# The last two row tiles as a block pair, with their conversions moved, in a quantised feed-forward kernel

## Chip, cores and metric

One core of a Trainium2 chip. The metric is the device time of one execution in microseconds (us), the median of several runs.

## The reference

The input `x` has 2 x 2048 rows of 512, in 32 tiles of 128 rows. For each batch element a weight matrix is mixed from eight, `x` is multiplied by it and a bias is added; the result goes through a gated feed-forward block whose three weight matrices are ternary and whose activations are rounded to 8 bits with a scale per row; the block's output is added to `x`.

```python
w_bot = einsum('bg,got->bot', cond_8, weight * mask)
h = einsum('bnt,bot->bno', x, w_bot) + bias
act_quant(v): s = 127 / max|v| over the row;  round(v * s) / s
weight_quant(w): s = 1 / mean|w|;  clip(round(w * s), -1, 1) / s
gate = silu(act_quant(h) @ weight_quant(w_gate).T)
up = act_quant(h) @ weight_quant(w_up).T
out = x + act_quant(gate * up) @ weight_quant(w_down).T
```

## The kernel before

Everything is written out by hand: five programs, one for each engine's queue (PE, DVE, ACT, POOL and SP), which meet through semaphores only. An instruction that waits holds up everything behind it on its engine.

**Conditioning (up to about 119 us).** For every row tile `h = x @ w_bot + bias` is formed in fp32. Tiles 0 to 7 are done plainly: four products of 128 x 512 a tile (`cond_products`, L1126), then on DVE the bias sum, the largest absolute value of each row and two small operations (`cond_tile`, L871 to L879), then on ACT rounding (L546, adding and later taking away the constant ROUND) and conversion to fp16 (L541), then a DMA transpose by SP into `qT` (L256). Tiles 8 to 29 go as eleven *block pairs* (`pair_product`, L1308): two tiles and the halves of their matrices are multiplied as a 2 x 2 block product with seven block products instead of eight, each two instructions of 128 x 256 columns. For this POOL forms four sums of the input blocks (`pair_sum`, L414), ACT puts the bias into PSUM (`seed_bias`, L557) and copies the first product (`copy_first`, L564), and DVE adds shared parts between products (`pair_share` L891, `pair_seed` L898, `pair_c22` L904) and takes the largest values of both tiles in one reduction (`pair_largest`, L911). The weights are made ternary beside it: scaling on POOL (L398) or, for w_down, on ACT (`scale_down`, L568), then two passes on DVE (`ternary_piece`, L862 and L864), four pieces for each matrix.

Tiles 30 and 31 (`LATE` = 30) are not part of this. Their products are plain, eight slices that are put between the chunks of steps 0 to 2.

**Steps 0 to 31 (from 119 us).** Step s takes tile s through gate and up: four chunks of 512 columns, each a gate product (L1164), an up product (L1171), a SiLU on ACT (`silu_chunk`, L593) and a multiplication on DVE (`product`, L988). DVE then reduces the largest value (`largest`, L1006), forms the scale (L1048, L1051, L1053), and ACT rounds the tile (`round_tile`, L623) and converts it in two halves (`convert`, L640). SP transposes each half into `q2T` (L321). From step 6 on the gate side too is done in block pairs (L1206). The down products (L1236) go as block pairs of two tiles, seven products spread over the following steps; their sums of blocks are formed on DVE (`add_blocks`, L954) as soon as both tiles are transposed, and four combinations of w_down's blocks are formed once on POOL (L446 to L451, into `combo`). Then POOL has two unit columns (`unit_of`, L455), eight combinations of w_gate's blocks for each half (`combine_gate`, L372 to L377), and for every step the unit, the sums of `qT` blocks (L493) and the output tile (L462 to L473). DVE's scale (L1048) of step s waits for the unit of step s - 2.

**The end.** Tile 30 and tile 31 are multiplied by w_down plainly (`down_plain` L1243, `down_cut` L1253), between the last products of pair 14. Tile 30 is rounded in two halves (`round_half`, L629); the first is converted on POOL (`convert_first_half`, L498), the second on ACT. Tile 31 is rounded on DVE (L1060) and converted on ACT.

## Time and profile before

| | us |
|---|---|
| median of 3 runs | 440.59 |
| lowest and highest run | 439.86 to 440.75 |
| the profiled execution, its own time | 440.59 |
| span of the profiled execution | 438.8 |
| PE busy in the span | 425.5 |
| DVE, ACT, POOL busy | 363.5, 336.8, 205.3 |

The span runs from the first to the last instruction that the profiler recorded; 1.8 us of the execution's own time lie around it. PE is TensorE, DVE VectorE, ACT ScalarE, POOL GpSimd, SP the engine that issues most DMAs. In a timeline row stand the start in us from the span's start, the duration, the engine, the line, the operation and its operands; in square brackets the time for which the engine had nothing to do before, and what ended it. An fp32 product stands there as two instructions.

### The profile page before, as it was taken

To read this page: it belongs to the slowest core of one execution; us is meant where nothing else is said; L and a number is where in the kernel's file an instruction comes from. 1 tells how busy PE (TensorE), PEld (TensorE's weight loads), DVE (VectorE), ACT (ScalarE), POOL (GpSimd) and SP (SyncE) were. 2 spreads that over 40 slices of the span, in tenths; PEclk is the share of its full clock that TensorE was granted. 3 is DMA by queue.
4 is the path that set the end of the run, shared out by engine and by line. 5 is a ranking of instruction groups with operands and counts; after the bars stand their busy time and mean duration, and the time that the engine had idled before them with its cause. 6 is when DMAs were issued, how large, how long until landed. Compare 5 with 4: busy or idle time off the path is not lost.

```text
span 438.8 us, 7668 instructions
## 1 busy us (share of the span) xinstructions
PE 425.5 (97%) x2318; PEld 257.5 (59%) x2318; DVE 363.5 (83%) x611; ACT 336.8 (77%) x474; POOL 205.3 (47%) x221
## 2 busy tenths in 40 slices
PE   4899999999999999999999999999999999999997
PEld 0234688888744455556555565655566555556555
DVE  0327768898897988899999999899999999899992
ACT  1215988778867976888888888888888888888871
POOL 0006999999149995142432423344142333414132
PEclk9999999999999999999999999999999999999999
DMA  7999999995142337254453635535263553535375
GB/s 277 404 396 408 308 335 339 313 251 144 36 98 48 61 66 187 48 145 85 134 120 73 146 70 143 97 118 120 76 157 64 135 115 100 120 87 142 80 162 154
DMA packets 104458, 69.79 MB, mean 159 GB/s; under 512 B 87280, under 2 KB 87536, under 8 KB 102896
## 3 DMA queue, kind: packets, MB, share of 16 engines
q1 hardware_dynamic: 103712, 67.13, 56.9%
q10 hardware_dynamic: 720, 2.36, 1.5%
q8 instruction: 11, 0.18, 0.2%
q14 instruction: 15, 0.12, 0.1%
HBM read 40.11 MB, written 8.39 MB: 111 GB/s over the span
## 4 chain that ended last, share of the span: by engine, by line
PE 59%; DMA 14%; issue 11%; DVE 9%; ACT 5%; POOL 1%; DVEq 0%; ACTq 0%; SPq 0%; POOLq 0%
PE ps L1308 15%; DMA wc<-wc 12%; PE ps L1171 11%; PE ps L1236 10%; PE ps L1126 8%; PE ps L1206 8%; PE ps L1164 4%; ACT wc L640 3%; DVE wc L954 3%; DVE wc L988 2%; DMA wc<-wcond 2%; PE ps L1139 2%; DVE p_part L1006 1%; ACT result L660 1%; PE ps L1243 1%
## 5 line engine op out<-in xcount | busy, mean ns | idle before, releaser
L1171 PE MATMUL ps<-tern_up,qT 128*128 128x512 f16 x512 | 131.1, 379 | 0.0
L1171 PEld LDWEIGHTS ps<-tern_up,qT 128*128 (+1 forms) x512 | 50.0, 98 | 54.5 <-DVE wc L988 0.4
L1006 DVE TENSOR_REDUCE p_part<-wc 128x1 f32<-128x1536 f32 x64 | 77.9, 1217 | 1.7
L988 DVE TENSOR_TENSOR wc<-ps,xT_sb 128x512 f32<-128x512 f32 x104 | 71.1, 683 | 7.3 <-issue 3.3
L640 ACT ACTIVATE wc<-wc 128x1024 f16<-128x1024 f32 x63 | 66.0, 1051 | 4.1 <-DMA wc<-wc 2.1
L623 ACT ACTIVATE wc<-wc,p_scale 128x2048 f32<-128x2048 f32 x30 | 60.1, 2002 | 4.3 <-DVE p_scale L1053 4.3
L1236 PE MATMUL ps<-wc 128*128 128x256 f16 x480 | 62.2, 273 | 0.7 <-DVE wc L954 0.7
L954 DVE TENSOR_TENSOR wc<-wc 128x1024 f16<-128x1024 f16 x60 | 56.9, 949 | 4.5 <-DMA wc<-wc 3.6
L1236 PEld LDWEIGHTS ps<-wc 128*128 128x128 f16 x480 | 46.9, 98 | 18.6 <-issue 1.2
L455 POOL TENSOR_SCALAR out_unit<-p_max,up_step,w_mean 128x1 f32<-128x1 f32 x32 | 11.3, 355 | 99.2 <-DVE p_max L1048 99.2
L618 ACT ACTIVATE xT_sb<-ps,gate_unit 128x512 f32<-128x512 f32 x78 | 49.2, 683 | 10.9 <-PE ps L1206 10.4
L462 POOL TENSOR_TENSOR result<-result,x_res 128x512 f32<-128x512 f32 x15 | 19.1, 1273 | 73.3 <-issue 73.3
L1236 PE MATMUL ps<-tern_down,wc 128*128 128x256 f16 x360 | 46.7, 273 | 0.6 <-ACT ps L653 0.5
L1236 PEld LDWEIGHTS ps<-tern_down,wc 128*128 128x128 f16 x360 | 35.1, 98 | 14.6 <-ACT ps L653 0.7
L1126 PE MATMUL ps<-w_bot,xT_sb 128*128 128x512 f32 x80 | 36.7, 597 | 1.6 <-DVE w_bot L845 1.6
L1206 PE MATMUL ps<-tern_gate,qT 128*128 128x512 f16 x104 | 26.7, 379 | 0.0
L1126 PEld LDWEIGHTS ps<-w_bot,xT_sb 128*128 128x128 f32 x80 | 14.9, 190 | 19.6 <-issue 15.9
L593 ACT ACTIVATE wc<-ps,gate_unit 128x512 f32<-128x512 f32 x24 | 16.2, 683 | 12.6 <-PE ps L1164 12.6
L837 DVE SCALAR_TENSOR_TENSOR w_bot<-ps,half_on,w_bot 128x512 f32<-128x512 f32 x8 | 6.0, 747 | 23.4 <-PE ps L1139 23.4
L1164 PE MATMUL ps<-tern_gate,qT 128*128 128x512 f16 x96 | 24.6, 379 | 0.0
L765 ACT ACTIVATE w_bot<-ps,half_on 128x512 f32<-128x512 f32 x8 | 5.1, 683 | 25.5 <-PE ps L1139 25.5
L1206 PE MATMUL ps<-xT_sb,w_bot 128*128 128x512 f16 x78 | 23.2, 379 | 0.0
(142 smaller groups left out, 778.3 us busy)
## 6 DMA issues: line engine op xcount, KB each, us to landing
xT_sb<-xT SPq DMA_DIRECT2D x32, 256.0 KB, 6.6
x_res<-x SPq DMA_DIRECT2D x30, 256.0 KB, 2.9
out<-result SPq DMA_DIRECT2D x29, 256.0 KB, 2.4
wc<-wcond SPq DMA_DIRECT2D x12, 512.0 KB, 13.4
wc<-w_gate SPq DMA_DIRECT2D x4, 1024.0 KB, 16.0
wc<-w_up SPq DMA_DIRECT2D x4, 1024.0 KB, 8.4
wc<-w_down SPq DMA_DIRECT2D x4, 1024.0 KB, 6.1
wc<-wcond ACTq DMA_DIRECT2D x4, 512.0 KB, 7.7
```

The source lines that it names most:

```text
L618: nc.scalar.activation(gsilu[:, q, i % 2], source, ACT.Silu, scale=unit_column(s + i // 2)).then_inc(gsilu_ready[q], 1)
L623: nc.scalar.activation(prod[:, par], prod[:, par], ACT.Copy, bias=ROUND, scale=p_scale[:, par:par + 1]).then_inc(p_rounded, 1)
L640: nc.scalar.activation(q2[:, 1024 * half:1024 * half + 1024], prod[:, par, 1024 * half:1024 * half + 1024], ACT.Copy, bias=-ROUND).then_in ...
L954: nc.vector.tensor_tensor(qsum[:, i], in0, in1, op).then_inc(sum_ready, 1)
L988: nc.vector.tensor_tensor(prod[:, par, 512 * i:512 * i + 512], ps[:, UP + i % 2], source, ALU.mult).then_inc(prod_ready, 1)
L1006: nc.vector.tensor_reduce(p_part[:, par, i:i + 1], prod[:, par, 512 * lo:512 * hi], AX.X, ALU.max, apply_absolute_value=True).then_inc(par ...
L1126: ins = nc.tensor.matmul(ps[:, cond_bank(t)], xT_sb[:, t % XSLOTS, k], w_bot[:, t // HALF, k], start=(k == 0), stop=(k == KH - 1))
L1164: ins = nc.tensor.matmul(ps[:, bank], tile_of(s, k), tern_gate[:, i, k], start=(k == 0), stop=(k == KH - 1))
L1171: ins = nc.tensor.matmul(ps[:, UP + i % 2], tile_of(s, k), tern_up[:, i, k], start=(k == 0), stop=(k == KH - 1))
L1206: ins = nc.tensor.matmul(ps[:, bank], tile, weight, start=(i < 2 and k == 0), stop=(k == 1), skip_group_check=(i >= 2))
L1236: ins = nc.tensor.matmul(ps[:, bank, 0:NB], tile, weight, start=(i < 2 and k == 0), stop=(k == KB - 1), skip_group_check=(i >= 2))
L1308: ins = nc.tensor.matmul(place, tile, weight, start=(i == 0 and k == 0), stop=(k == 1), skip_group_check=(i > 0))
```

## The change

Tiles 30 and 31 become block pair 15 (`LAST_PAIR`), with its seven products in the seven slots after chunks (0, 1) to (1, 3) of steps 0 and 1. They use PSUM banks 2 and 3. So POOL forms four sums more ahead of the combinations of w_down; ACT seeds the bias before step 0, copies the first product in step 0, rounds both tiles at the end of step 2 and converts them in steps 3 and 4; DVE has the pair's shared sum in step 0, its seed and last block in step 1 and its largest values in step 2. The rounding of tile 29 goes ahead of step 0, the scaling of w_down's piece 3 behind the last SiLU of step 0 and its ternary passes to the end of DVE's step 0. Tile 1 is rounded between the first and the second SiLU of step 2. The transposes of tiles 30 and 31 go two steps later on SP's queue, and the two first loads of `x_res`, whose memory now holds sums of pair 15, into step 2. At the end POOL converts both halves of tile 30, and ACT rounds its first half before `scale_c21` and does the last SiLU of step 31 after `copy_shared`.

```diff
+LAST_PAIR = HALF - 1
+LAST_PAIR_SLOTS = {(0, 1): 0, (0, 2): 1, (0, 3): 2, (1, 0): 3, (1, 1): 4, (1, 2): 5, (1, 3): 6}
...
@sync, for s in range(1, TILES):
-                if s in (2, 3):
-                    transpose_q(LATE + s - 2)
+                if s == 2:
+                    sp.wait_ge(cond_psum, TILES)
+                    for t in range(2):
+                        sp.dma_start(x_res[:, t], x[t]).then_inc(s_xres[t], 16)
+                if s in (4, 5):
+                    transpose_q(LATE + s - 4)
...
@gpsimd
             last_sums(14)
+            first_sums(LAST_PAIR)
+            last_sums(LAST_PAIR)
...
-                        convert_first_half(LATE)
+                        convert_half(LATE, 0)
+                        convert_half(LATE, 1)
...
@scalar, odd_step(s)
-                            silu_block(g, q, i)
+                            if not (s == TILES - 1 and i == 3 and q == 1):
+                                silu_block(g, q, i)
...
+                if s == TILES - 1:
+                    round_half(s - 1, 0)
                 if s >= 5:
                     scale_c21(j - 1)
...
                 else:
-                    round_half(s - 1, 0)
                     round_half(s - 1, 1)
...
+                    if s == 3:
+                        last_convert(0)
                 else:
                     if s == TILES - 1:
-                        convert(s - 1, 0, 1)
+                        silu_block(g, 1, 3)
                     copy_seed(j)
...
-                if s == 1:
-                    cond_round(LATE)
...
@scalar, even_step(s)
                     silu_chunk(s, 0)
+                    if s == 2:
+                        round_tile(s - 1, 1)
                     silu_chunk(s, 1)
-                if s > 0:
+                if s > 0 and s != 2:
                     round_tile(s - 1, 1)
...
                 if s == 0:
-                    pair_round(PAIR_END - 1, 1)
                     pair_round(PAIR_END - 1, 0)
-                    pair_convert(PAIR_END - 1)
+                    copy_first(LAST_PAIR)
...
                     silu_chunk(s, 3)
+                if s == 0:
+                    scale_down(3)
+                    pair_convert(PAIR_END - 1)
                 if s == 2:
-                    cond_round(LATE + 1)
+                    pair_round(LAST_PAIR, 1)
+                    pair_round(LAST_PAIR, 0)
+                if s == 4:
+                    last_convert(1)
...
             pair_convert(PAIR_END - 2)
-            scale_down(3)
+            pair_round(PAIR_END - 1, 1)
+            seed_bias(LAST_PAIR)
             for s in range(0, TILES, 2):
...
@vector, step(s)
+                if isinstance(s, int) and s == 1:
+                    pair_seed(LAST_PAIR)
                 product(s, par, 0, g)
...
                 if isinstance(s, int) and s == 0:
+                    pair_share(LAST_PAIR)
                     ternary_piece(2, 2)
-                if late is not None:
-                    cond_tile(late)
+                if isinstance(s, int) and s == 2:
+                    pair_largest(LAST_PAIR)
...
                     product(s, par, 2, g)
-                if isinstance(s, int) and s == 0:
-                    ternary_piece(2, 3)
+                if isinstance(s, int) and s == 1:
+                    pair_c22(LAST_PAIR)
...
+                if isinstance(s, int) and s == 0:
+                    ternary_piece(2, 3)
...
@tensor
+                if first and i == 0:
+                    pe.wait_ge(h_rounded, TILES)
...
-                    if (s, c) in LATE_SLICES:
...
-                        cond_products(t, [k])
-            pe.wait_ge(h_rounded, LATE)
+                    if (s, c) in LAST_PAIR_SLOTS:
+                        pair_product(LAST_PAIR, LAST_PAIR_SLOTS[s, c])
```

ScalarE around steps 1 to 3, in the program before. L593 is a SiLU, L623 the rounding of a tile, L640 a conversion of half a tile, L546 and L541 rounding and conversion of tiles 30 and 31:

```order
L640 ACTIVATE wc<-wc 128x1024 [waits p_rounded]
L546 ACTIVATE h_sb<-h_sb,h_inv 128x512 [waits h_col]
L541 ACTIVATE q_sb<-h_sb 128x512 [waits s_qT2,h_rounded]
L593 ACTIVATE wc<-ps,gate_unit 128x512 [waits prod_ready,gate_psum] x2
L623 ACTIVATE wc<-wc,p_scale 128x2048 [waits p_col]
L593 ACTIVATE wc<-ps,gate_unit 128x512 [waits prod_ready,gate_psum]
L640 ACTIVATE wc<-wc 128x1024 [waits s_q2T0,p_rounded]
L640 ACTIVATE wc<-wc 128x1024 [waits s_q2T1,p_rounded]
L593 ACTIVATE wc<-ps,gate_unit 128x512 [waits prod_ready,gate_psum]
L546 ACTIVATE h_sb<-h_sb,h_inv 128x512 [waits h_col]
L541 ACTIVATE q_sb<-h_sb 128x512 [waits s_qT3,h_rounded]
```

The same place in the changed program, where L598 is the SiLU, L628 the rounding, L643 the conversion, and L575 the rounding of tiles 30 and 31:

```order
L643 ACTIVATE wc<-wc 128x1024 [waits p_rounded]
L598 ACTIVATE wc<-ps,gate_unit 128x512 [waits prod_ready,gate_psum]
L628 ACTIVATE wc<-wc,p_scale 128x2048 [waits p_col]
L598 ACTIVATE wc<-ps,gate_unit 128x512 [waits prod_ready,gate_psum] x2
L643 ACTIVATE wc<-wc 128x1024 [waits s_q2T0,p_rounded]
L643 ACTIVATE wc<-wc 128x1024 [waits s_q2T1,p_rounded]
L598 ACTIVATE wc<-ps,gate_unit 128x512 [waits prod_ready,gate_psum]
L575 ACTIVATE h_sb<-ps,h_inv 128x512 [waits q_ready,h_col] x2
L598 ACTIVATE wc<-ps,gate_unit 128x512 [waits prod_ready,gate_psum] x2
```

The rounding of tile 1 has moved one SiLU up, and rounding and conversion of tile 30 are gone from in front of it.

GpSimd in the last steps, in the changed program. L466 scales a part of the output tile, L498 converts half of tile 30 (before, one such row stood here), L473 adds `x_res`, L455 is a unit:

```order
L466 TENSOR_SCALAR result<-result,out_unit 128x256 [waits c22_done]
L498 TENSOR_SCALAR wc<-wc 128x1024 [waits s_q2T0,tail_rounded]
L498 TENSOR_SCALAR wc<-wc 128x1024 [waits s_q2T1,tail_rounded]
L473 TENSOR_TENSOR result<-result,x_res 128x512 [waits s_xres1,c22_scaled,c21_out]
L455 TENSOR_SCALAR out_unit<-p_max,up_step,w_mean 128x1 [waits p_col]
```

The second conversion, which was ScalarE's, stands between the first and the last sum of the output tile.

## Rows read from the trace of the kernel before

**Rows 1.** The page, busy time, share of the span and instructions of each engine
```profile
PE 425.5 (97%) x2318; PEld 257.5 (59%) x2318; DVE 363.5 (83%) x611; ACT 336.8 (77%) x474; POOL 205.3 (47%) x221
```

**Rows 2.** Timeline of TensorE, 108 to 166 us: start, duration, instruction, idle before
```profile
115.94 1.03 PE L1308 MATMUL ps<-gcombo,result 128*128 128x256 f32 x4
...
139.21 1.02 PE L1126 MATMUL ps<-w_bot,xT_sb 128*128 128x512 f32 x2
140.07 1.03 PE L1164 MATMUL ps<-tern_gate,qT 128*128 128x512 f16 x4
...
151.44 1.03 PE L1236 MATMUL ps<-wc 128*128 128x256 f16 x8 [0.73 <-DVE wc L954]
```

**Rows 3.** Timeline of ScalarE, steps 1 and 2
```profile
138.77 0.67 ACT L593 ACTIVATE wc<-ps,gate_unit 128x512 f32<-128x512 f32 x1
141.13 0.69 ACT L593 ACTIVATE wc<-ps,gate_unit 128x512 f32<-128x512 f32 x1 [1.69 <-PE ps L1164]
141.72 1.99 ACT L623 ACTIVATE wc<-wc,p_scale 128x2048 f32<-128x2048 f32 x1
...
144.18 2.00 ACT L640 ACTIVATE wc<-wc 128x1024 f16<-128x1024 f32 x2
```

**Rows 4.** The chain that ended last, 134 to 172 us: the transpose of tile 1
```profile
146.54 3.26 DMA wc<-wc
```

**Rows 5.** Timeline of VectorE, 100 to 160 us
```profile
106.25 1.74 DVE L862 TENSOR_SCALAR tern_up<-wc 128x2048 f16<-128x2048 f32 x1
...
112.16 1.22 DVE L862 TENSOR_SCALAR tern_down<-wc 128x2048 f16<-128x2048 f32 x1
...
130.53 0.69 DVE L988 TENSOR_TENSOR wc<-ps,wc 128x512 f32<-128x512 f32 x1
...
142.07 0.69 DVE L988 TENSOR_TENSOR wc<-ps,wc 128x512 f32<-128x512 f32 x1 [1.90 <-PE ps L1171]
142.68 0.68 DVE L871 TENSOR_TENSOR h_sb<-ps,bias_sb 128x512 f32<-128x512 f32 x1
...
148.31 0.27 DVE L1048 TENSOR_SCALAR p_max<-p_part,p_floor 128x1 f32<-128x1 f32 x1
...
149.89 1.40 DVE L954 TENSOR_TENSOR wc<-wc 128x1024 f16<-128x1024 f16 x1 [0.28 <-DMA wc<-wc]
```

**Rows 6.** Costliest groups: the largest values of a pair; busy, mean ns, idle before
```profile
L911 DVE TENSOR_REDUCE h_max<-ps 128x2 f32<-128x1024 f32 x11 | 13.4, 1215 | 1.2 <-PE ps L1308 1.1
```

**Rows 7.** Line L954 over the whole span: shortest, median and longest in ns
```profile
L954 DVE TENSOR_TENSOR wc<-wc x60: 677/693/1793, 149.9 to 428.3; 128x1024 f16<-128x1024 f16 x60
```

**Rows 8.** Timeline of GpSimd, 100 to 160 us
```profile
111.23 0.73 POOL L414 TENSOR_TENSOR result<-xT_sb,result 128x256 f32<-128x256 f32 x1
127.01 4.07 POOL L446 TENSOR_TENSOR wc<-tern_down 128x2048 f16<-128x2048 f16 x1 [15.06 <-DVE tern_down L864]
...
143.27 0.67 POOL L455 TENSOR_SCALAR out_unit<-p_max,up_step,w_mean 128x1 f32<-128x1 f32 x2
...
149.59 1.16 POOL L373 TENSOR_TENSOR gcombo<-tern_gate 128x512 f16<-128x512 f16 x1
```

**Rows 9.** Timelines at the end; the last row gives a transpose's us to landing
```profile
425.94 3.63 PE L1243 MATMUL ps<-tern_down,wc 128*128 128x512 f16 x16 [0.43 <-DMA wc<-wc]
...
431.17 1.92 PE L1253 MATMUL ps<-tern_down,wc 128*128 128x256 f16 x16
...
419.40 1.15 ACT L629 ACTIVATE wc<-wc,p_scale 128x1024 f32<-128x1024 f32 x1
...
421.23 0.99 DVE L954 TENSOR_TENSOR wc<-wc 128x1024 f16<-128x1024 f16 x1
...
420.64 1.04 POOL L498 TENSOR_SCALAR wc<-wc 128x1024 f16<-128x1024 f32 x1 [1.68 <-ACT wc L629]
...
427.92 1.23 SPq L321 DMA_TRANSPOSE wc<-wc  x1
...
wc<-wc SPq DMA_TRANSPOSE x1, 3.2
```

51 lines of the change are left out of this document (20 added, 31 removed).

## The prediction

> **What bounds the kernel now.** I read the page's busy shares first, then the timeline of each engine in the stretch the change touches (105 to 165 us) and at the end (415 to 439 us). TensorE is busy 97% of the span, at full clock [rows 1], so the kernel gets faster only if TensorE gets less to do or if one of its few pauses shrinks. Two pauses matter here.
>
> The first is at the first down product, `down_product(0, 0)`: it starts at 151.44, 0.73 us after TensorE ran dry, released by VectorE's L954 (`add_blocks`), which forms the sum that it multiplies [rows 2]. The sum starts at 149.89 [rows 5]. What stands behind it is a chain through four engines: SiLU of step 2, rounding of tile 1 at 141.72, its conversion at 144.18 [rows 3], then the transpose on SP's queue, whose second half needs 3.26 us from 146.54 and lands at 149.80 [rows 4].
>
> The second is at the end: tile 30's plain down products start at 425.94 after 0.43 us of waiting for a transpose [rows 9]. But the tile 31 products behind them start at 431.17, and the transpose they need was issued at 427.92 and takes 3.2 us, so it lands at 431.12 [rows 9]. That is a second limit, which the first pause hides.
>
> **The change, part by part.**
>
> *Work removed from TensorE.* Tiles 30 and 31 took eight slices like the one at 139.21, which holds TensorE until the next product at 140.07: 0.86 us each [rows 2]. A block pair takes seven products, each four instructions of the duration shown at 115.94 (1.03 us as a group, as the slice has 1.02) [rows 2], so 0.86 each as well. One slot goes: **-0.86 us** from 139.21 on. The seven slots are the first seven of the old eight. They come every three products, 2.59 us, so counted back from 139.21 the fifth stands at 131.46. What they wait for comes in time: bias seed and copy are issued a chunk ahead of their slots. `pair_seed` on VectorE is the tight one: it comes right after the step that ended at 130.53 [rows 5] plus 0.5 for what is added there, and would end at about 131.4, with its slot at 131.46. I take 0 for it and 0.1 as its upper bound.
>
> *Four GpSimd sums more (L414, tiles 30 and 31).* Before, GpSimd is done at 111.96 (0.73 us from 111.23 [rows 8]) and VectorE's ternary piece at 112.16 takes 1.22 us; the same piece at 106.25, with GpSimd at work, takes 1.74 [rows 5]. The new sums put the piece at 112.16 into the second case: +0.52, and its second pass some 0.3 more. Little of it arrives: TensorE's product at 115.94 [rows 2] waits for VectorE's seed, which had about 0.7 us in hand. I count **+0.1**.
>
> *Tile 1 rounded sooner.* ScalarE's SiLU at 138.77 was held up by tile 30's conversion, which is gone; rounding can follow it at about 139.14 instead of 141.72, and lasts 1.9. So the SiLU at 141.13 [rows 3], which TensorE would now allow at 140.27, still comes only at about 141.04. VectorE's product that reads it starts near 141.77, where it was 142.07 [rows 5]. This is where most of the freed slot is lost: -0.3 in place of -0.86. In the order on VectorE the four instructions of `cond_tile` from 142.68 on [rows 5] give way to `pair_largest`, whose large reduction takes 1.215 us [rows 6] where the bias sum and reduction of `cond_tile` took about as much: 0. The conversions come 1.4 us sooner, and the second half of the transpose, at 3.26 us [rows 4], lands near 148.3. The sum at 149.89 [rows 5] had stood 0.3 us behind its product for that landing; it now starts right after the product, at 149.2 to 149.35: some 0.6 sooner.
>
> *GpSimd's queue.* The scaling of the fourth w_down piece goes behind the last SiLU of step 0, and its ternary piece behind VectorE's step 0. That step ended at 130.53 with the piece inside [rows 5]; with `pair_share` in it too the piece now ends near 131.1. GpSimd's four combinations of w_down, which waited for it until 127.01 [rows 8], start 4.1 us later. They take 16.26 us together (127.01 to 143.27 [rows 8]), and `unit_of(0)` then ends at about 147.8 instead of 143.6. VectorE's p_max of step 2 waits for that unit: it stood at 148.31 [rows 5] and would now stand at 147.96. The cover is 0.2 us. The gate combinations, behind it in the queue, come 4.1 later too and end near 168.3, with their readers on TensorE at 170: 0, with about 1 us of cover.
>
> *Who is first at 149.3.* VectorE's L954 takes 0.69 us as a rule and up to 1.79 [rows 7]. At 149.89 it took 1.40, while GpSimd ran an instruction from 149.59 for 1.16, to 150.75 [rows 5, 8]; it ended 0.54 after GpSimd's did. At the end it is the same again: GpSimd to 421.68, VectorE's add from 421.23 for 0.99, to 422.22, also 0.54 later [rows 9]. In the new order the GpSimd instruction starts at 149.15 to 149.3 and VectorE's at 149.2 to 149.35. If GpSimd is first, the sum ends near 150.9, 0.4 sooner than before: **-0.4**. If VectorE is, it takes 0.69 and ends near 150.0; then TensorE's own queue is the limit, at 150.3: **-1.14**. The Trainium skill (SBUF — State Buffer, section Who interferes with whom) says that a VectorE instruction with two SBUF inputs contends with a GpSimd one that reads SBUF, and that "whoever issues first gets the shared pair for the whole instruction". The trace agrees, with 1.40 against 0.69. By it nothing lies between the two values; without it I would have kept 1.40 us and said -0.55.
>
> *Tile 30 converted on GpSimd.* ScalarE rounds the first half about 0.9 us sooner, since a SiLU and a scaling no longer stand ahead of it (it was at 419.40, 1.15 us [rows 9]). The first half's transpose is then out 0.9 us sooner, and the pause of 0.43 at 425.94 goes. Only 0.3 of this or less can reach the end, as tile 31's transpose lands at 431.12 whatever tile 30 does. That transpose hangs on VectorE's chain of products and sums, of which the add at 421.23 is a link. Now GpSimd's second conversion (1.04 us, as the first at 420.64 [rows 9]) starts near 421.1, and VectorE's add at 421.23. GpSimd first: the add ends at 422.14 + 0.54 = 422.68 instead of 422.22, and the whole end moves by **+0.46**. VectorE first: 0.69 instead of 0.99, **-0.3**. The moved SiLU costs nothing: its reader on VectorE stands behind a reduction of 1536 columns that comes after this add, and at most the 0.6 us of the SiLU itself if that cover were gone. The moved transposes and loads (tiles 30 and 31, x_res) stand on SP's queue where it is idle, and their readers come 15 us later: 0, at most 0.3 for the transpose of tile 1 beside the loads.
>
> *Sum.* The profiled execution took 440.59, which is also the median. With one race each way: -0.4 + 0.1 - 0.3 = -0.6, or -1.14 + 0.1 + 0.46 = -0.6. Forecast **440.0 us**.
>
> **Rivals.**
>
> *Both races go to VectorE*: each sum takes 0.69 us, as most of the 60 do [rows 7], and -1.14 + 0.1 - 0.3 = -1.3 gives 439.2 us. For it: the starts are estimated within 0.1 us of each other. Against it: both estimates put GpSimd just ahead. The Trainium skill's rule of the shared pair, named above, speaks for such an outcome as much as for its opposite, since the one that is first waits for nothing.
>
> *Both go to GpSimd, nothing is gained*: -0.4 + 0.1 + 0.46 = +0.2, 440.7 us. The slot is saved but stays as waiting. For it: the estimates; against it: an add that starts 0.1 us earlier turns it.
>
> *GpSimd's queue becomes the bound (slower).* Place: p_max of step 2. The cover is 0.2 us; each combination of w_down that GpSimd starts late, or that runs longer than 4.07 us, goes through p_max to the product, the sum and the first down product, microsecond for microsecond. If the four run 0.4 longer each, +1.6 less 0.2 of cover: +1.4 on a sum of -0.1, 441.9 us. It decides from about 1.2 us of lateness (slower by over 0.2%). For it: GpSimd had no pause from 127 to 167, and the change adds 4.1 us of lateness. Against: between 131 and 147 VectorE has no instruction of the kind that stretched at 106.25 or 149.89.
>
> *The change does not do what it says*: the pair does its seven products in their slots, but one waits (`pair_seed`, copy of the first product) and the slot saved is spent there: 440.6 us, no change.
>
> **How the numbers follow.** About 0.2% (0.9 us) is what a measurement of this kernel can tell from no change. Chances: forecast case 0.42, both to VectorE 0.22, both to GpSimd or the slot spent 0.29, GpSimd's queue 0.07. Single runs before spread from 439.86 to 440.75, so I let a case reach 0.4 us to either side. The range goes from 439.0 (both to VectorE, with spread) to 441.0 (both to GpSimd, with spread); beyond it lies most of the GpSimd rival. Faster by over 0.2% means below 439.7: most of the VectorE case (0.20) and over a fourth of the forecast's own (0.12), 0.32. Slower means above 441.5: the GpSimd rival, 0.07. Within: 0.61.
>
> **What would show it.** Seven products between 121 and 138, with `down_product(0, 0)` at 150.3 to 151.1. p_max of step 2 with no wait for GpSimd; if it waits more than 0.2 us, the slower rival is on. The first sum of `add_blocks` either 0.7 or about 1.6 us long, nothing between; likewise the second sum of pair 14 at the end. Tile 30's down products without a pause, and a pause of up to 0.9 us ahead of tile 31's. The forecast is wrong if the steps 6 to 29 in the loop change their length, which nothing here touches.

## The result, and the profile after

The change makes the kernel slower: **442.42 us** (median of 15 executions, 440.75 to 445.42) against 440.55 for the kernel before on the same chip (15 executions, 439.86 to 441.12). The ratio is 1.0048, with a 95% interval from 1.0031 to 1.0065. The forecast was 440.0, with a range to 441.0. The profiled execution of the change took 443.89, 3.3 us more than that of before (440.59). It is the third longest of the fifteen, so it holds more losses than the median execution has.

The page gives no hint of the cause. TensorE is busy 0.7 us longer than in [rows 1], at full clock, with twelve instructions more of either kind (products and weight loads); VectorE is busy 0.9 longer, ScalarE 0.6, GpSimd 5.5.

```profile
PE 426.2 (96%) x2330; PEld 259.3 (59%) x2330; DVE 364.4 (82%) x610; ACT 337.4 (76%) x475; POOL 210.8 (48%) x226
```

TensorE's waits over the whole span tell more (engine, line, what it waited for; us in total, times, longest). The first and the third stand at the start of the kernel, which is as before. The kernel before has one wait of L1236, the line that is now L1256, for VectorE (0.7); here are three, and new ones for L911 and for a transpose of tile 31.

```profile
PE ps L1157 <- DMA wc<-wcond: 6.2, 2, 5.5
PE ps L1256 <- DVE wc L967: 1.9, 3, 0.8
PE ps L1144 <- DVE w_bot L858: 1.6, 1, 1.6
PE ps L1328 <- DVE ps L911: 1.0, 1, 1.0
PE ps L1256 <- ACT ps L656: 0.5, 1, 0.5
PE ps L1263 <- DMA wc<-wc: 0.5, 1, 0.5
PE ps L1273 <- DMA wc<-wc: 0.3, 1, 0.3
PE ps L1189 <- DVE wc L1001: 0.2, 1, 0.2
```

They stand in TensorE's timeline at these places. Line numbers have moved: L1236 is L1256, L1308 is L1328, L954 is L967, L1243 is L1263.

```profile
117.20 1.13 PE L1328 MATMUL ps<-gcombo,result 128*128 128x256 f32 x4 [0.96 <-DVE ps L911]
...
150.79 1.04 PE L1189 MATMUL ps<-tern_up,qT 128*128 128x512 f16 x4 [0.23 <-DVE wc L1001]
152.37 1.03 PE L1256 MATMUL ps<-wc 128*128 128x256 f16 x8 [0.54 <-DVE wc L967]
...
194.31 1.03 PE L1256 MATMUL ps<-wc 128*128 128x256 f16 x8 [0.75 <-DVE wc L967]
...
233.24 1.05 PE L1256 MATMUL ps<-wc 128*128 128x256 f16 x8 [0.65 <-DVE wc L967]
...
426.26 1.05 PE L1256 MATMUL ps<-tern_down,wc 128*128 128x256 f16 x8 [0.46 <-ACT ps L656]
428.63 3.63 PE L1263 MATMUL ps<-tern_down,wc 128*128 128x512 f16 x16 [0.45 <-DMA wc<-wc]
434.32 1.92 PE L1273 MATMUL ps<-tern_down,wc 128*128 128x256 f16 x16 [0.32 <-DMA wc<-wc]
```

The last instruction of the computation on VectorE starts at 438.90 here and at 435.75 before: 3.15 us later. I took each pause as the start of a row less the start and the occupied time of the rows ahead of it (0.216 us a 512-column product). In order of time the profiled execution has: 0.13 later by 110; +1.24 at the fifth product of pair 14 (117.20); -0.86 for the slot; +0.09 at the slot after `pair_seed`; +0.28 more than before around the first down product (0.19 + 0.39 + 0.72 against 0.11 + 0.91); **+0.92 at 194.31 and +0.81 at 233.24**, where the kernel before has no pause at all between 162 and 423; +0.03 at 428.63; +0.49 at 434.32. The sum is 3.13.

The largest parts are the early pause and the two pauses in the loop. The first I had not foreseen at its size, the others not at all.

**The early pause** lies in VectorE's queue. L911 is the seed that the product at 117.20 waits for. Rows of VectorE, then of GpSimd, in the change:

```profile
112.30 1.56 DVE L875 TENSOR_SCALAR tern_down<-wc 128x2048 f16<-128x2048 f32 x1
113.90 1.10 DVE L877 TENSOR_SCALAR tern_down<-tern_down 128x2048 f16<-128x2048 f16 x1
114.93 0.70 DVE L938 TENSOR_SCALAR gate_unit<-h_unit,w_mean 128x16 f32<-128x16 f32 x1
115.54 0.77 DVE L941 TENSOR_SCALAR up_step<-h_unit,w_mean 128x16 f32<-128x16 f32 x1
...
116.72 0.43 DVE L911 TENSOR_TENSOR ps<-ps,w_bot 128x256 f32<-128x256 f32 x1
```
```profile
112.92 1.53 POOL L412 TENSOR_TENSOR x_res<-x_res,xT_sb 128x256 f32<-128x256 f32 x1
114.42 1.18 POOL L412 TENSOR_TENSOR x_res<-xT_sb 128x256 f32<-128x256 f32 x1
115.55 0.74 POOL L412 TENSOR_TENSOR x_res<-xT_sb,x_res 128x256 f32<-128x256 f32 x1
```

The two unit steps L938 and L941 work on 16 columns and take 0.23 us each without GpSimd beside them (rows below, from an experiment); here each waits out a GpSimd sum and takes 0.70 and 0.77. The slowed pair of ternary passes is as I said, the unit steps I had not counted. The GpSimd sums themselves stretch too, from 0.73 to 1.53 and 1.18.

**The pauses in the loop** lie in a stretch whose code the change leaves as it was. At 232.50 the first sum of blocks on VectorE comes after 2.05 us of waiting for a transpose; at 192.39 it comes late in the same way, and then starts 0.04 us behind a GpSimd addition and takes 1.78 where 0.69 is its time alone.

```profile
192.39 1.78 DVE L967 TENSOR_TENSOR wc<-wc 128x1024 f16<-128x1024 f16 x1 [1.06 <-issue]
...
232.50 0.69 DVE L967 TENSOR_TENSOR wc<-wc 128x1024 f16<-128x1024 f16 x1 [2.05 <-DMA wc<-wc]
```
```profile
192.35 1.27 POOL L473 TENSOR_TENSOR result<-result,x_res 128x512 f32<-128x512 f32 x1
```

The transposes themselves are late: those of `wc` issued at 186.8, 188.1 and 227.4 land after 4.2 to 4.9 us, all others of `wc` from 160 to 390 after 3.0 to 3.7. What lies beside them is seen in the view of DMA work, here for 3.2 us in 40 slices of 0.08 (busy tenths of the 16 DMA engines, then GB/s). First the kernel before, from 186.0, with the transposes of the same step; then the change, from 187.5.

```profile
DMA  0000000000000599999999999999835999999999
GB/s 0 0 0 0 0 0 0 0 0 0 0 0 10 109 205 224 224 214 230 195 237 186 227 192 214 198 186 176 174 74 106 189 237 205 240 218 195 224 182 214
...
wc<-wc SPq DMA_TRANSPOSE x2, 3.1
```
```profile
DMA  0000095999999999000000010000000079999999
GB/s 0 0 0 0 0 237 128 205 208 211 198 218 189 144 61 22 0 0 0 0 0 0 3 10 6 10 10 10 10 10 10 10 147 291 278 291 301 260 244 285
...
q1 hardware_dynamic: 1219, 0.30, 103.4%
q8 instruction: 1, 0.02, 2.7%
...
wc<-wc SPq DMA_TRANSPOSE x2, 4.3
```

Before, the two transposes follow one another without a hole. In the change there is a hole of 1.3 us from 188.8 to 190.1, and in this window lies one transfer of the queue "instruction", 16,384 bytes. By the trace it starts at 188.0 and takes 1.37 us of one DMA engine (2.7% of 16 engines over 3.2 us). The other engines finish their part of the first transpose by 188.8 and stop. From 189.3, when the load is through, packets move again, but at a pace of one engine only: the next view, from 189.4 to 190.1, has 34 of them in 0.7 us, where sixteen engines moved about 80 in each 0.1 us ahead of the hole. Only then, at 190.1, does the second transpose start on all engines. The view doesn't name the engines. I read it so: the one engine that has the load to move does its part of the transpose late, which holds up the transpose as a whole and the next one behind it.

```profile
DMA  2010101101011011011010110110110110100005
...
q1 hardware_dynamic: 34, 0.01, 9.3%
```

The kernel before has eleven such loads, the change has eleven too. By the trace's starts of transfers, in us of the span:

```
before  36.2 69.5 92.9 124.8 153.5 171.1 193.5 210.1 231.8 403.2 422.9
change  35.8 69.3 92.4 125.3 145.3 172.3 188.0 214.0 230.3 400.2 426.5
```

They are TensorE's program. Between the first and the ninth load of the kernel before, TensorE begins 2072 instructions by the trace (products, weight loads and the sequencer's own), 259 a load; VectorE begins 61 and ScalarE 46 a load. There are none while the loop repeats the same code (232 to 403), and the kernels below with 226 to 256 instructions more on TensorE have twelve loads in place of eleven. The Trainium skill (Runtime: NRT & Kernel Launch, section Instruction fetch mechanics) says that the sequencer refills its memory "in 16 KiB blocks (256 instructions)" through a DMA queue of its own, and that crossing a boundary is "mostly hidden". The size agrees with the trace. That it is hidden holds for TensorE, which does not stop at 188.0; it does not hold for the transposes beside it, which take 1.1 us longer than before.

The loads that fell at 193.5 and 231.8 before, clear of the loop's transposes, fall at 188.0 and 230.3 in the change. The theory that I tested was that the added instructions move them. I took the change to add 13 instructions to TensorE's program. That count was wrong: the trace of the change has 5,086 instructions of TensorE, that of before 5,061, so it adds **25** (twelve products, twelve weight loads and one wait). The experiments named after 13, 242 and 243 instructions must be read with this number. The first four were made before I had the theory.

### The profile page after: what moved, and what is told of

Its sections match the earlier page's. It is cut to its first block, busy times and chain, and to the rows that moved or that the text cites. A ratio compares the mean times of both kernels' runs of the same rounds, so it can differ in the third digit from the quotient of the medians.

```text
span 441.9 us, 7708 instructions
## 1 busy us (share of the span) xinstructions
PE 426.2 (96%) x2330; PEld 259.3 (59%) x2330; DVE 364.4 (82%) x610; ACT 337.4 (76%) x475; POOL 210.8 (48%) x226
## 4 chain that ended last, share of the span: by engine, by line
PE 80%; DMA 6%; DVE 6%; issue 4%; ACT 3%; ACTq 0%; DVEq 0%; SPq 0%
PE ps L1189 20%; PE ps L1256 17%; PE ps L1328 16%; PE ps L1224 15%; PE ps L1144 6%; DMA wc<-wc 4%; PE ps L1182 3%; DMA wc<-wcond 2%; PE ps L1157 2%; ACT wc L643 2%; DVE wc L967 1%; DVE wc L1001 1%; DVE p_part L1019 1%; PE ps L1273 1%; ACT xT_sb L623 0%
## 5 line engine op out<-in xcount | busy, mean ns | idle before, releaser
L643 ACT ACTIVATE wc<-wc 128x1024 f16<-128x1024 f32 x62 | 65.0, 1051 | 4.3 <-DVE wc L1078 2.1
L1256 PE MATMUL ps<-wc 128*128 128x256 f16 x480 | 62.2, 273 | 1.9 <-DVE wc L967 1.9
L628 ACT ACTIVATE wc<-wc,p_scale 128x2048 f32<-128x2048 f32 x30 | 60.1, 2002 | 4.7 <-DVE p_scale L1069 4.7
L967 DVE TENSOR_TENSOR wc<-wc 128x1024 f16<-128x1024 f16 x60 | 56.2, 936 | 8.0 <-DMA wc<-wc 5.6
L1256 PEld LDWEIGHTS ps<-wc 128*128 128x128 f16 x480 | 46.7, 98 | 20.3 <-issue 2.2
L623 ACT ACTIVATE xT_sb<-ps,gate_unit 128x512 f32<-128x512 f32 x78 | 49.3, 684 | 11.7 <-PE ps L1224 11.2
L455 POOL TENSOR_SCALAR out_unit<-p_max,up_step,w_mean 128x1 f32<-128x1 f32 x32 | 11.4, 357 | 95.7 <-DVE p_max L1064 95.7
L462 POOL TENSOR_TENSOR result<-result,x_res 128x512 f32<-128x512 f32 x15 | 19.1, 1273 | 73.3 <-issue 73.3
L1256 PE MATMUL ps<-tern_down,wc 128*128 128x256 f16 x360 | 46.7, 273 | 0.6 <-ACT ps L656 0.5
L1256 PEld LDWEIGHTS ps<-tern_down,wc 128*128 128x128 f16 x360 | 35.1, 98 | 14.6 <-ACT ps L656 0.7
L1144 PE MATMUL ps<-w_bot,xT_sb 128*128 128x512 f32 x64 | 28.5, 599 | 1.6 <-DVE w_bot L858 1.6
L1328 PE MATMUL ps<-w_bot,xT_sb 128*128 128x256 f32 x96 | 24.7, 380 | 0.0
L598 ACT ACTIVATE wc<-ps,gate_unit 128x512 f32<-128x512 f32 x24 | 16.4, 686 | 9.7 <-PE ps L1182 9.6
L473 POOL TENSOR_TENSOR result<-result,x_res 128x512 f32<-128x512 f32 x15 | 22.7, 1514 | 2.2 <-ACT result L676 2.2
```

Of the source, the lines that this page charges most:

```text
L623: nc.scalar.activation(gsilu[:, q, i % 2], source, ACT.Silu, scale=unit_column(s + i // 2)).then_inc(gsilu_ready[q], 1)
L628: nc.scalar.activation(prod[:, par], prod[:, par], ACT.Copy, bias=ROUND, scale=p_scale[:, par:par + 1]).then_inc(p_rounded, 1)
L643: nc.scalar.activation(q2[:, 1024 * half:1024 * half + 1024], prod[:, par, 1024 * half:1024 * half + 1024], ACT.Copy, bias=-ROUND).then_in ...
L967: nc.vector.tensor_tensor(qsum[:, i], in0, in1, op).then_inc(sum_ready, 1)
L1144: ins = nc.tensor.matmul(ps[:, cond_bank(t)], xT_sb[:, t % XSLOTS, k], w_bot[:, t // HALF, k], start=(k == 0), stop=(k == KH - 1))
L1256: ins = nc.tensor.matmul(ps[:, bank, 0:NB], tile, weight, start=(i < 2 and k == 0), stop=(k == KB - 1), skip_group_check=(i >= 2))
```

## The experiments

Each kernel was timed in turn with the kernel before; its own median is given beside that of before on the same chip.

### The sums of pair 15 after the unit steps

```diff
+            pool.wait_ge(units_ready, 4)
             first_sums(LAST_PAIR)
```

> The changed kernel, but GpSimd starts its four new sums only after VectorE's unit steps (one wait more on GpSimd). Theory of the shared port: in the changed kernel VectorE's ternary piece (1.56 + 1.10 us) and two unit steps (0.70, 0.77 us) stand in the way of pair 14's seed, which TensorE misses by 1.1 us at 117.2. Here the piece takes 1.22 + 0.69, the steps 0.23 each, TensorE's pause goes, and the median falls by about 1.1 us, to 441.3. If the end is set by GpSimd's lateness (units and gate combinations come after w_down's four), the early 1.1 us is given back later, as the combinations start the same distance behind VectorE, and the median stays within 0.4 of 442.4.

Measured: 441.50 us (440.31 to 444.05, 12 executions) against 440.23; ratio 1.0036 (1.0022 to 1.0051). The early pause is gone, and VectorE's four instructions have their short times:

```profile
111.64 1.22 DVE L876 TENSOR_SCALAR tern_down<-wc 128x2048 f16<-128x2048 f32 x1
112.89 0.69 DVE L878 TENSOR_SCALAR tern_down<-tern_down 128x2048 f16<-128x2048 f16 x1
113.50 0.23 DVE L939 TENSOR_SCALAR gate_unit<-h_unit,w_mean 128x16 f32<-128x16 f32 x1
113.64 0.23 DVE L942 TENSOR_SCALAR up_step<-h_unit,w_mean 128x16 f32<-128x16 f32 x1
```

The place of that pause and what makes it are seen in the rows, but not its price in the median. Against before on the same chip the median lies 1.27 us higher, where that of the change lies 1.87 higher, and the two intervals (1.0022 to 1.0051, 1.0031 to 1.0065) overlap widely. Nor does every execution have the pause: of the seven traces that form these sums in the early place, three have it (the change and the next two experiments) and four don't. In those four GpSimd is one sum further on and has none beside the unit steps, which take 0.22 or 0.23 us.

### The kernel before with the four sums, unused

```diff
             last_sums(14)
+            first_sums(15)
+            last_sums(15)
...
+            sp.wait_ge(x_sum_ready, 48)
             for t in range(2):
                 sp.dma_start(x_res[:, t], x[t])
```

> The kernel before with one thing added: GpSimd forms the four block sums of tiles 30 and 31 right after pair 14's, and nobody uses them (work added, nothing left out; SP waits for them ahead of the x_res loads). Theory of the shared port: the whole early loss comes from these four sums alone: TensorE pauses about 1.1 us before pair 14's fifth product, and of it 0.9 to 1.1 reach the end: 441.5. If the loss needs the other moves around step 0, it stays at 440.6.

Measured: 440.21 (439.82 to 442.31, 12 executions) against 440.23; ratio 1.0004 (0.9994 to 1.0014). I had expected 441.5, which is a miss. The profiled execution was the longest of the twelve, 442.31, and has the early pause with the rows as in the change (1.56, 1.10, 0.77); nine of the twelve took 439.82 to 441.02. So the four sums cost about 1.2 us in an execution in which GpSimd's and VectorE's instructions meet, and the times of most executions leave no room for that. It looks like a race and not like a fixed price; only one execution was traced.

### The end as before

Tile 30's second half is converted on ScalarE again, the rounding and the last SiLU stand in their old places.

```diff
                         convert_half(LATE, 0)
-                        convert_half(LATE, 1)
...
-                if s == TILES - 1:
-                    round_half(s - 1, 0)
...
-                        silu_block(g, 1, 3)
+                        convert(s - 1, 0, 1)
```

> The changed kernel with its end as before: ScalarE rounds both halves of tile 30 together and converts the second one, GpSimd only the first. Theory of the shared port: VectorE's second sum of pair 14 goes from 1.47 back to 0.99 us, tile 31's down products start 0.46 sooner, median 442.0 (-0.45). If the conversion on GpSimd helps through the earlier transpose, the kernel gets slower, by up to 0.4 (442.8).

Measured: 442.11 (441.01 to 444.41, 10 executions) against 440.23; ratio 1.0039 (1.0021 to 1.0056). From the second product of pair 14 to the start of tile 31's products it takes 7.58 us, against 8.06 in the change and 7.57 before: the end of the change costs 0.5 us in the trace, as one side of the race in the prediction had it. The median does not show it: it lies 1.88 above before, that of the change 1.87. Two pauses stand in the loop (0.85 near 232, 0.93 near 404).

### w_down's last piece early

`scale_down(3)` and the ternary passes go back to their place ahead of step 0's end.

```diff
             seed_bias(LAST_PAIR)
+            scale_down(3)
...
+                if isinstance(s, int) and s == 0:
+                    ternary_piece(2, 3)
                 if isinstance(s, int) and s == 1:
```

> The changed kernel with w_down's last piece scaled ahead of step 0 and made ternary in the middle of VectorE's step 0, as before, so that GpSimd's combinations start 4 us sooner. If GpSimd's late queue costs anything (rival in the prediction), p_max of step 2 and the group products of step 5 get cover back and the median falls by 0.3 or more. By the shared port theory the lateness costs nothing, only the phase at the first sum of the down products changes (0.7 to 1.6 us long): 442.4, within 0.5 either way.

Measured: 441.97 (440.71 to 443.45, 10 executions) against 440.23; ratio 1.0032 (1.0020 to 1.0045). The median lies 1.74 above before, against 1.87, so GpSimd's later combinations are not the cause. In the trace with the sums late, which keeps the change's order of that queue, the first `unit_of` ends near 147.3 (two take 0.65 from 146.93), and p_max starts at 147.58 behind VectorE's own reduction (146.78 + 0.69): the cover that the prediction gave as 0.2 was there.

The three of these that keep TensorE's program as the change has it took 441.50 to 442.11; the kernel before with the four sums, which has the old program, took 440.21. That led to the loads, and to the next run.

### The kernel before, with 13 idle instructions in TensorE's program

Two waits in the kernel's text become one instruction on the chip: this trace has 5,074 instructions of TensorE, 13 more than before. That is about half of what the change adds.

```diff
-            pe.wait_ge(mix_w_ready, 3)
+            for _ in range(2 * 13 + 1):
+                pe.wait_ge(mix_w_ready, 3)
             mix_products(0)
```

> The kernel before, with 13 instructions more at the start of TensorE's program, where it waits 4.7 us for the first load: waits on a semaphore that has long been reached, the same number that the change adds to this program. No other engine's work differs. Theory of the code loads: the 16 KB loads of TensorE's program move as they do in the change, to about 187 and 228 us, beside the DMA transposes of wc, of which some five each take 4.0 to 4.9 us in place of 3.0 to 3.2; TensorE pauses 0.5 to 0.9 after one or both of them (near 193 and 232), and the median is 440.8 to 441.7 against 440.2. Rival, that the slow transposes come with the change's order of work or with GpSimd's new instructions: nothing moves, every transpose of the loop takes 3.0 to 3.5, no pause, 440.0 to 440.4.

Measured: **442.01** (440.42 to 443.11, 12 executions) against 440.22; ratio 1.0032 (1.0016 to 1.0048). Thirteen instructions that wait for nothing, at the start where TensorE waits for data anyway, make the kernel before about as slow as the change. They delay the first product by 1.08 us (6.52 against 5.44), which is made up by the second (8.18 against 8.15). The loads moved, but not to where I expected: the one of 153.5 is at 146.9, those of the loop at 195.3, 211.8 and 233.1, which is 1.3 to 1.8 later, about as much as TensorE is late there (1.7), and still clear of the transposes. The price is paid at the first down product, whose transposes take 4.1 in place of 3.1 to 3.3. The views are DMA work from 146.0 in slices of 0.08, then VectorE, then TensorE:

```profile
DMA  0000000000090389999999980000000010000999
GB/s 0 0 0 0 0 0 0 0 0 0 0 205 0 77 179 214 221 208 195 202 176 90 38 3 0 0 3 6 6 10 10 6 13 10 10 6 16 211 288 294
...
q8 instruction: 1, 0.02, 2.5%
```
```profile
151.37 1.65 DVE L954 TENSOR_TENSOR wc<-wc 128x1024 f16<-128x1024 f16 x1 [1.13 <-DMA wc<-wc]
```
```profile
153.17 1.03 PE L1236 MATMUL ps<-wc 128*128 128x256 f16 x8 [1.83 <-DVE wc L954]
```

The same hole, and a wait of 1.83 where it was 0.73 [rows 2]: 1.1 us of the 1.9 by which this execution is longer. The rest is 0.27 in the first 33 us and 0.33 between 72 and 79, in gaps of 0.1 to 0.3 that I can't put down to anything.

### The change moved by about a whole load, partly at the start

With its own 25 these 243 instructions make 268, twelve more than one load holds.

```diff
+            def fill(n):
+                for _ in range(2 * n):
+                    pe.wait_ge(mix_w_ready, 3)
...
+                    if t < SEEDED:
+                        fill(6)
...
+            fill(32)
             mix_products(0)
+            fill(19)
             early_products(0, range(FIRST))
```

> The change, with 243 satisfied waits more in the first 50 us of TensorE's program, so that with the change's own 13 instructions its program is moved by 256 instructions of 64 bytes, one load of 16 KB, and the loads fall in the same places of the loop as in the kernel before. Theory of the code loads: the transposes near 187 and 228 us take 3.0 to 3.3 again, the pauses near 194 and 233 (0.92 and 0.81 in the change) are gone, and the median falls from 442.4 to 440.9 to 441.6. What stays is the pause near 117, where it comes, and the end. If the waits hold up the first 50 us, that shows as a later start of the pair products and is taken off. Rival: 442.2 to 442.6, pauses as in the change.

Measured: 443.02 (442.10 to 445.75, 8 executions) against 440.22; ratio 1.0067 (1.0044 to 1.0089). A miss as a timing: the waits at the start hold TensorE up (the first pair product starts at 54.1 in place of 49.4). As a trace it went the way of the theory: no transpose of `wc` from 160 to 420 took more than 3.7, and the pauses at 194 and 233 are gone. One of 0.81 stands at 387, with no load beside it.

### Both partial undoings, without and with that move

Edits: those of the first and third experiment; then those and the one above.

> The change with both partial undoings together: the four sums of pair 15 only after VectorE's unit steps, and the end in the old order (tile 30 converted by ScalarE and VectorE as before). If the two terms add up: 441.5 with the sums alone and 442.1 with the old end alone, against 442.4, make 441.2. Theory of the code loads: the rest above 440.2, less the 0.86 saved, is the pauses at 194 and 233, so 441.0 to 441.5. Rival, that the new order of the first steps costs by itself: also 441.2, but without pauses in the loop.

> Both partial undoings and the moved code loads in one. What is left of the change is the pair product in place of two plain tiles (0.86 saved) and the two small pauses near 151 and 152 (1.1 together, of which about 0.9 the kernel before has too in another place). Theory of the code loads: no pause in the loop, median 439.5 to 440.3, at or below the kernel before. Rival, that the loop's pauses have another cause: 441.2 as without the move.

Measured: 442.19 (439.56 to 444.49, 12 executions) and 444.34 (442.75 to 447.24, 6 executions) against 440.22; ratios 1.0037 (1.0021 to 1.0053) and 1.0077 (1.0055 to 1.0099). Both are misses. The first should have been 441.2 by adding the two parts: its profiled execution, 444.49, is the longest of the twelve and has four pauses in the loop, 1.16 near 212, 0.80 near 232, 0.80 near 385 and 0.92 near 405. Here are their rows, with the wait that the profile puts down to VectorE:

```profile
212.30 1.05 PE L1256 MATMUL ps<-wc 128*128 128x256 f16 x8 [0.99 <-DVE wc L967]
232.17 1.05 PE L1256 MATMUL ps<-wc 128*128 128x256 f16 x8 [0.64 <-DVE wc L967]
...
385.49 1.05 PE L1256 MATMUL ps<-wc 128*128 128x256 f16 x8 [0.64 <-DVE wc L967]
405.48 1.03 PE L1256 MATMUL ps<-wc 128*128 128x256 f16 x8 [0.75 <-DVE wc L967]
```

The other traces' transposes of 4 us and more, and their loads, are in the table further down. In the second experiment the work stood 3.5 to 4 us later for the slow start while the loads did not move by the same amount, and two met the transposes at 210 and 230 (4.8 to 4.9). Parts that shift the loads cannot be added up.

### The move without cost at the start: before, change, and change with both undoings

The filling waits now stand only between fp32 products, which leave the queue time (7 or 8 ahead of each from 15 us on, one ahead of the products of the first ten pairs but their first).

```diff
+                    if t < SEEDED and ks != [0]:
+                        fill(7)
...
+                if r < PAIR0 + 10 and i > 0:
+                    fill(1)
```

> Control for the next two: the kernel before, with 256 satisfied waits more in TensorE's program, exactly one code load of 16 KB, set between the f32 matmuls of 15 to 80 us, which take 0.22 or 0.43 each and leave the queue time. Nothing at the start. Theory of the code loads: the loads fall where they fell (about 153.6, 171, 194, 210, 232), no transposes of the loop beyond 3.5, median 440.0 to 440.8; what it lies above 440.2 is the price of the filling itself. Rival, that more instructions cost by their number: 441 to 442, as with the 13.

> The change, with 242 satisfied waits set in the same way, so that TensorE's program stands within one instruction of a whole code load from the kernel before. With 243 of them, partly at the start, the transposes of the loop were at 3.0 to 3.4 and the loop's pauses near 194 and 233 were gone, but the start lost 4.7 us by 54 and the total could not tell. Theory of the code loads: transposes near 187 and 228 at 3.0 to 3.4, no pauses there, median 440.6 to 441.6 against 442.4 (the control's own price is taken off). Rival, that the loop's pauses belong to the change's order: 442.2 to 442.8 with pauses of 0.8 to 0.9.

> The change with the sums of pair 15 after the unit steps, the old end, and the same 242 filling waits. Theory of the code loads: what is left is the saved slot (0.86) against the later first product of the down stage (0.93 later than before, of which the plain kernel's own pause is part): no pauses in the loop, median 439.6 to 440.6 against 442.2 unfilled. Rival: 441.8 to 442.4.

Measured, against 439.96 for before (29 executions):

| kernel | median us (range, n) | ratio (95%) |
|---|---|---|
| before, 256 more | 440.77 (439.57 to 441.78, 12) | 1.0013 (1.0002 to 1.0025) |
| change, 242 more | 440.81 (439.64 to 442.71, 12) | 1.0022 (1.0008 to 1.0036) |
| change, sums late, old end, 242 more | 440.52 (439.80 to 441.03, 12) | 1.0010 (1.0001 to 1.0019) |

In both versions of the change the filling makes the median fall, though the order of work is the same. The cleanest pair is the change with the sums late and the old end, since there the sums start only behind the unit steps, filled or not: without filling 442.19, which is 1.97 above before (ratio 1.0021 to 1.0053), with it 440.52, 0.56 above (1.0001 to 1.0019). The intervals don't touch; 1.4 us go. Its four pauses in the loop become one, of 0.64 at 383. **So idle instructions in TensorE's program, with no work altered, are worth more than 1 us.** That they act through the loads alone is not shown: the filling also makes the products at 15.6 us 1.1 us late, and they are level with the kernel before only near 104, so the engines may meet one another differently behind it.

For the change itself it is less clear. It goes from 1.87 above before to 0.85, but the intervals (1.0031 to 1.0065, 1.0008 to 1.0036) touch, and its filled trace has no early pause either. The kernel before, filled in the same way, stands 0.81 above, so between the filled kernels nothing is left of the difference. Nor are the loads of the filled change back in place, since 25 + 242 is 267, 11 more than one load: they are at 189.3 and 227.6, clear of the transposes. In this trace the products that follow 191 and 229 start without a wait, and TensorE waits for nothing between 160 and 420:

```profile
191.09 1.03 PE L1195 MATMUL ps<-tern_up,qT 128*128 128x512 f16 x4
191.95 1.04 PE L1262 MATMUL ps<-wc 128*128 128x256 f16 x8
```
```profile
229.22 1.03 PE L1195 MATMUL ps<-tern_up,qT 128*128 128x512 f16 x4
230.08 1.04 PE L1262 MATMUL ps<-wc 128*128 128x256 f16 x8
```

The control was meant to stay at 440.0 to 440.8 and did, at the upper end. Its own rise of 0.8 is not the filling's time, since its products stand at 104.5 as before; the filling moved the load of 153.5 to 149.2, onto the second transpose of the first down product (4.8), with a wait of 1.86 there in place of 0.73 [rows 2].

### The last three

The earlier rounding of tile 1 is undone, alone and with the two other undoings, both with 242 filling waits. The third experiment keeps the rounding of the change, has the two other undoings and 16 filling waits fewer: 226 and 25 are 251, five fewer than one load, the nearest of all versions to the kernel before.

```diff
-                    if s == 2:
-                        round_tile(s - 1, 1)
...
-                if s > 0 and s != 2:
+                if s > 0:
```

> The change with the code loads back in place (440.8 without the next edit), and tile 1 rounded where the kernel before rounds it. My theory: the first sums of tile 0's and 1's blocks come about 0.6 later and the first down product with them, so the pauses near 149 and 151 (0.40 and 0.70) move but don't shrink in sum by more than 0.3: median 440.7 to 441.4. Rival, that the earlier rounding is what costs, since it brings GpSimd's and VectorE's instructions to the same start near 149: 440.0 to 440.4.

> The same with the sums of pair 15 late and the old end. My theory: 440.4 to 441.0 against 440.5 without this edit. Rival, that the earlier rounding costs: 439.6 to 440.1.

> As late_tail_spread242 (440.5), with 16 filling waits fewer, which puts each code load some 1.2 us later: to about 148, 169, 194, 211 and 232. Theory of the code loads: they stay in the hollows between the transposes of the loop except the one near 148, so 440.2 to 440.9, with the pauses near 149 and 151 as they were (they come from VectorE's sum behind GpSimd's instruction) and that near 383 in some runs only. If the loop's transposes slow again to 4 and over with a load beside them, up to 441.5. Rival, that the place of the loads doesn't matter within 1 us: 440.5 to 0.2.

Measured, against 440.48 (29 executions): 440.75 (439.76 to 443.10, 12), 440.82 (439.79 to 441.60, 11) and 440.70 (440.20 to 441.96, 11); ratios 1.0013 (0.9998 to 1.0028), 1.0007 (0.9996 to 1.0018), 1.0006 (0.9996 to 1.0015). None differs from before. The earlier rounding of tile 1 is worth nothing that these runs can tell: the two pauses ahead of the first down product are 0.34 and 0.98 without it, 0.40 and 0.71 with it. With 16 waits fewer the loads fell at 152.4, 170.4, 193.1, 212.0 and 233.2, each within 2 us of its place in the kernel before, and no transpose of `wc` took 4 us. No version beats the kernel before.

### All traces side by side

In the last column stands the median, and behind it how far it lies above that of before on the same chip. The profiled execution is one of six to fifteen, and often not like the median one.

| kernel | loads near 147, 188, 212, 230 | transposes of `wc` of 4.0 us and more, by issue (140 to 410) | TensorE's waits 160 to 420 | profiled execution, us | median us |
|---|---|---|---|---|---|
| before | 153.5, 193.5, 210.1, 231.8 | none | none | 440.6 | 440.2 |
| before, four sums | 154.6, 194.1, 213.7, 233.4 | none | none | 442.3 | 440.2 (0.0) |
| before, 13 more | 146.9, 195.3, 211.8, 233.1 | 145.9, 147.2 | none | 442.5 | 442.0 (1.8) |
| before, 256 more | 149.2, 193.5, 213.0, 232.7 | 146.4 | none | 441.8 | 440.8 (0.8) |
| change | 145.3, 188.0, 214.0, 230.3 | 186.8, 188.1, 227.4, 398.2 | 1.4 in 2 | 443.9 | 442.4 (1.9) |
| sums late | 143.5, 186.5, 211.5, 227.3 | 184.9, 394.6 | none | 440.3 | 441.5 (1.3) |
| old end | 145.0, 188.2, 213.0, 229.1 | 186.4, 187.8, 226.2, 397.0 | 1.4 in 2 | 443.1 | 442.1 (1.9) |
| w_down early | 144.0, 187.2, 211.8, 228.0 | 185.4, 186.7, 225.2, 396.7, 398.2 | 2.1 in 3 | 443.5 | 442.0 (1.7) |
| sums late, old end | 144.0, 186.6, 209.0, 229.1 | 185.5, 186.8, 206.2, 226.2, 398.0, 399.4 | 3.0 in 4 | 444.5 | 442.2 (2.0) |
| change, 243 more | 150.0, 196.9, 212.3, 231.3 | 147.4, 148.7 | 0.6 in 1 | 445.3 | 443.0 (2.8) |
| sums late, old end, 243 more | 150.5, 193.5, 212.9, 233.0 | 147.8, 149.1, 210.1, 230.2 | 2.3 in 3 | 447.2 | 444.3 (4.1) |
| change, 242 more | 146.3, 189.3, 214.4, 227.6 | 143.7, 145.0 | none | 440.8 | 440.8 (0.9) |
| sums late, old end, 242 more | 146.3, 193.1, 209.4, 230.7 | 143.7, 144.9 | 0.6 in 1 | 440.9 | 440.5 (0.6) |
| the same, 226 more | 152.4, 193.1, 212.0, 233.2 | none | 0.6 in 1 | 441.1 | 440.7 (0.2) |
| old rounding, 242 more | 145.0, 192.5, 208.9, 230.1 | 143.8, 145.1 | 0.6 in 1 | 440.9 | 440.8 (0.3) |
| sums late, old end and rounding, 242 more | 144.7, 192.4, 208.8, 230.0 | 143.7, 145.0 | none | 439.8 | 440.8 (0.3) |

That a load and a slow transpose go together is clear. The sixteen traces have 1,024 transposes of `wc` over the whole span. Of these 943 have no load between issue and landing, and none took more than 3.7 us; 54 took 4.0 or more, and each of them has a load there. The other 27 had a load there and took less (3.0 to 3.9), so these traces have no delay of that size without a load, but a load alone is not enough.

The kernel before has such a pair too, just outside the table: the two transposes ahead of its pause at tile 30's products, issued at 421.8 and 423.0, took 4.1 and 3.9 us with the load of 422.9 beside them. Where no load meets them, as in the change with 242 more, they take 3.0 to 3.1 and that pause is gone.

Two further steps are looser. *From a slow transpose to a wait of TensorE:* between 160 and 410 the traces have 17 groups of slow transposes, and TensorE waits behind 11 of them. With the sums late it waits behind neither, though the transpose issued at 184.9 took 4.4. There the sum that needed it was out ahead of GpSimd's addition, while in the change it started behind it (192.39, above):

```profile
190.20 0.88 DVE L968 TENSOR_TENSOR wc<-wc 128x1024 f16<-128x1024 f16 x1 [0.73 <-issue]
```
```profile
190.50 1.72 POOL L474 TENSOR_TENSOR result<-result,x_res 128x512 f32<-128x512 f32 x1
```

The slow transposes issued near 144 in the kernels with 242 more cost nothing that shows either: the same kernel with 226 has none, and the same first down product (150.85 against 150.89). *From the length of the program to the place of a load:* it is not the count alone. The five kernels with the change's own program for TensorE have their fourth load anywhere from 119.1 to 127.2 us.

The wait of 0.6 at 383 in the row of 242 more, with the sums late and the old end, has no load beside it: there the transposes took 3.0, and VectorE's sum started 0.03 us behind GpSimd's addition and waited it out. Such a wait between 382 and 390 is in seven of the twelve traces of the change and its variants, and in none of the four of the kernel before and its variants. Why, stays open; all the kernels run the same code there.

## Why the prediction was wrong

*Steps 6 to 29, "which nothing here touches".* This step failed, and with it the forecast, which put nothing for them: the profiled execution loses 1.73 us there, in the pauses at 194 and 233. I costed TensorE's new instructions by their time and not by their place in the program. With nothing altered but 242 idle instructions, the version with the sums late and the old end goes from 1.97 above before to 0.56, and the change from 1.87 to 0.85. I took the landing of a transpose as a constant too, though the one of 3.26 us at 146.54 [rows 4] comes just ahead of the sum that needs it, so that what lengthens it can be paid at once, as it was with 13 instructions more (+1.1).

*Four GpSimd sums, +0.1.* Mis-sized, not misplaced, where they meet VectorE at all. The rows said 0.52 + 0.3 against 0.7 of cover; what I left out are the two unit steps in the same queue, +0.47 and +0.54. Together 1.8 against the cover, and 1.24 arrived in the profiled execution. With the sums alone in the kernel before, the median paid nothing.

*The slot, -0.86.* Right. By `pair_seed`, 0 to 0.1: it was 0.09.

*Tile 1 rounded sooner, and the race near 149.* GpSimd was first, and the sum took 1.57 us where 1.6 was forecast for that case. The step said that -0.4 of the slot's -0.86 would arrive, so 0.46 would be taken back. Measured is 0.28, in pauses of 0.19, 0.39 and 0.72 where before had 0.11 and 0.91. The first down product stands at 150.5 to 151.1 in the traces with the new rounding and neither the early pause nor a late start, 0.4 to 0.9 ahead of [rows 2]. Right in size, though not for my reason: with the old rounding it stands at 150.2 and 150.3. And the sum has lengths between 0.7 and 1.6 after all: 0.88 in the row of 190.20 above, and 0.99 in [rows 9].

*GpSimd's queue, 0 with 0.2 of cover.* Right; the slower rival built on it was not what made the kernel slower.

*The end, +0.46 with GpSimd first.* Right in place and size: L967 at 423.89 takes 1.47 where it took 0.99 [rows 9], since it starts while GpSimd converts.

```profile
423.89 1.47 DVE L967 TENSOR_TENSOR wc<-wc 128x1024 f16<-128x1024 f16 x1
```
```profile
422.38 2.45 POOL L498 TENSOR_SCALAR wc<-wc 128x1024 f16<-128x1024 f32 x2 [0.76 <-ACT wc L634]
```

*The pause at tile 30's products goes.* Wrong in this execution (0.62 at 428.63), where its transposes took 4.9 and 4.3 beside the load at 426.5; in the change with 242 more it is gone, and the wait stands in front of tile 31 (0.98), as forecast. I had read the pause in the kernel before as a matter of when ScalarE rounds. Its transposes were slow ones, beside the load of 422.9.

So with its loads clear of the loop's transposes the change takes 440.8, near the rival in which both races go to GpSimd (440.7); that the numbers are so close is partly luck, since the fill moves other pauses as well. What I had no term for, 1.0 to 1.4 us in the medians, is more than the whole gain of 0.6 that I forecast. What of the remaining 0.8 above the plain kernel before is the end or the fill, these runs bound but don't divide: with the sums late and the old end it is 0.6, with 16 waits fewer 0.2.

## What to carry to other kernels

An edit that adds or removes instructions can move the later code loads of that engine, and a load that fell on DMA transposes here went with 1 to 2 us more for each of them. Whether the kernel pays depends on what waits for the transpose. Before costing a change of less than 1%, look in the DMA view for the queue "instruction" and note where its loads lie between transposes that are waited for. Then time the kernel with a few different lengths of idle filling in that engine's program, and count the added instructions in the trace and not by hand: a difference that goes with the filling is not the change's. And where GpSimd and VectorE slow each other, count every instruction of the stretch, the smallest too: those of 16 columns lost 0.47 and 0.54 us here, those of 2048 columns 0.34 and 0.41.
